# Six transposing DMAs per context in place of three, each issued after its predecessor has landed

## What is computed

```python
Pn = rmsnorm(P, input_norm_w)
k_proj, v_proj = Pn @ Wk.T, Pn @ Wv.T
for _ in range(3):
    q_proj = rmsnorm(slots, slot_norm_w) @ Wq.T
    scores = einsum('bkd,bmd->bkm', q_proj, k_proj) * SCALE
    attn = softmax(scores, axis=-2)
    attn = attn / (sum(attn, axis=-1) + EPS)
    slots = gru_cell(einsum('bkm,bmd->bkd', attn, v_proj), slots, ...)
```

## Time and profile before

| What | Value |
|---|---|
| median of 3 runs | 926.16 us (922.39 to 926.95) |
| span of the profiled execution, first to last instruction | 920.0 us |
| mean granted TensorE clock | 0.931 |
| PE busy | 771.6 us, 84% of the span |
| DVE busy | 599.2 us, 65% |
| ACT busy | 365.1 us, 40% |
| SP's DMA queue | 168272 packets, 100.85 MB |

### The profile page before, as it was taken

One profiled execution on the slowest core, in us unless ns is written; L12 is line 12 of the kernel. 1 busy time (PEld: TensorE's weight loads), 2 busy tenths in 40 slices (PEclk: granted clock), 3 DMA queues, 4 the chain that ended last, 5 costly groups with the idle time before them and its releaser, 6 DMA issues. The chain is left out here.

```text
span 920.0 us, 37878 instructions
## 1 busy us (share of the span) xinstructions
PE 771.6 (84%) x17278; PEld 644.6 (70%) x17278; DVE 599.2 (65%) x1152; ACT 365.1 (40%) x732; POOL 161.6 (18%) x431
## 2 busy tenths in 40 slices
PE   5697689998979998979998989888689886749995
PEld 2545579898979998969998979787644764324442
DVE  3886446875866776766875775645565878783325
ACT  3874415333534333524333521101247763352321
POOL 3021110311320411320311311101001013140003
PEclk9898889999988999999999999989889788779998
DMA  9977970346192346192355290601394701543424
GB/s 339 379 151 135 254 132 5 55 80 178 14 202 98 56 75 183 26 186 102 56 81 178 36 200 9 138 6 41 101 372 114 227 21 24 196 142 93 122 78 149
DMA packets 179419, 115.75 MB, mean 126 GB/s; under 512 B 145788, under 2 KB 158132, under 8 KB 176060
## 3 DMA queue, kind: packets, MB, share of 16 engines
q1 hardware_dynamic: 168272, 100.85, 43.2%
q10 hardware_dynamic: 8988, 6.69, 2.4%
q0 software_dynamic: 2000, 5.80, 2.2%
HBM read 61.94 MB, written 12.85 MB: 81 GB/s over the span
## 5 line engine op out<-in xcount | busy, mean ns | idle before, releaser
L1036 PE MATMUL banks<-qa,ctxT 128*128 128x64 f16 x3744 | 124.3, 197 | 26.7 <-issue 14.4
L1036 PEld LDWEIGHTS banks<-qa,ctxT 128*128 128x128 f16 x3744 | 120.5, 101 | 28.9 <-issue 15.3
L987 PEld LDWEIGHTS banks<-wall,whhT 128*128 128x128 f16 x3456 | 110.5, 99 | 14.9 <-issue 7.9
L987 PE MATMUL banks<-wall,whhT 128*128 128x64 f16 x3456 | 113.0, 195 | 7.9 <-issue 6.4
L987 PE MATMUL banks<-qa,wall 128*128 128x64 f16 x3456 | 104.9, 193 | 3.1 <-DVE qa L787 2.8
L987 PEld LDWEIGHTS banks<-qa,wall 128*128 128x128 f16 x3456 | 102.5, 98 | 3.4 <-DVE qa L787 3.0
L1055 PE MATMUL banks<-qa,wall 128*128 128x64 f16 (+1 forms) x1872 | 91.6, 197 | 7.1 <-issue 5.7
L1055 PEld LDWEIGHTS banks<-qa,wall 128*128 128x128 f16 (+1 forms) x1872 | 90.9, 101 | 7.8 <-issue 7.8
L1055 PE MATMUL banks<-wall 128*128 128x64 f16 (+1 forms) x936 | 90.4, 197 | 0.0
L1055 PEld LDWEIGHTS banks<-wall 128*128 128x128 f16 (+1 forms) x936 | 86.1, 101 | 0.0
L552 ACT ACTIVATE wall<-wall 128x832 f32<-128x832 f32 x24 | 21.5, 897 | 141.3 <-DVE wall L749 141.3
(11 more groups left out here) (279 smaller groups left out, 1490.9 us busy)
## 6 DMA issues: line engine op xcount, KB each, us to landing
wall<-in_ctx_dram SPq DMA_DIRECT2D x17, 1024.0 KB, 10.5
wall<-in_L_ffn_routed_w_dram SPq DMA_DIRECT2D x23, 512.0 KB, 8.3
unit<-in_ctx_dram SPq DMA_DIRECT2D x6, 1024.0 KB, 7.6
xg_scratch<-room SPq DMA_DIRECT2D x1, 3840.0 KB, 20.7
y_scratch<-room ACTq DMA_DIRECT2D x15, 256.0 KB, 2.0
ctxT<-in_L_xattn_gru_wih_dram SPq DMA_DIRECT2D x3, 1024.0 KB, 17.5
ctxT<-in_L_xattn_gru_whh_dram SPq DMA_DIRECT2D x1, 3072.0 KB, 26.1
ctxT<-in_L_attn_Wqkv_dram SPq DMA_DIRECT2D x12, 256.0 KB, 7.2
```

The source lines that it names most:

```text
L987: mm = pe.matmul(dst[o], a, b, start=start, stop=True, skip_group_check=True)
L1036: mm = pe.matmul(score[n][:, t * K:(t + 1) * K], a, q, start=(k == 0), stop=(k == 3 * DC - 1), skip_group_check=True)
```

## The change

`TURNS` gets six pieces of 5, 4, 4, 4, 5 and 4 halves. Each piece after the first waits until the one before has landed. The second and third load of a context wait for the landing of the one before (for contexts from 2 on). The load of x is waited for before the next is issued, the slots' load before `Wqkv`; the twelve loads of `Wqkv` go out in pairs, each pair after all earlier ones have landed.

```diff
-TURNS = ((0, 9), (9, 17), (17, HALVES))
+TURNS = ((0, 5), (5, 9), (9, 13), (13, 17), (17, 22), (22, HALVES))
...
             def load_context(b, groups=(0, 1, 2)):
                 n_rows = dram.ctx[b]
+                before = 3 * (b // 3) - (b > 3 and b % 3 == 1)
                 for j in groups:
+                    if b >= 2 and j >= 1:
+                        sp.wait_ge(ctx_in[b % 3], 16 * (before + j))
...
                     sp.wait_ge(tile_low, b * MT + lows)
+                    if g >= 1:
+                        sp.wait_ge(tile_turned[n][g - 1], 16 * (b // 2 + 1))
...
             sp.dma_start(rows, ...).then_inc(big.x_in, 16)
+            sp.wait_ge(big.x_in, 16)
...
             sp.wait_ge(scored[0], PAIRS * ITERS)
+            sp.wait_ge(big.res_in, 16)
             load_wqkv(sp, dram, big)
...
         for ii in range(4):
+            if ii % 2 == 0 and 4 * s + ii >= 2:
+                sp.wait_ge(big.wqkv_in, 16 * (4 * s + ii))
```

## The result

The kernel after took 960.2 us, the median of 4 runs (959.53 to 964.35), against 924.27 us (918.74 to 926.95, 4 runs) for the kernel before: a ratio of 1.0393, 95% interval 1.0353 to 1.0433. The forecast was 955, with a range of 930 to 976. The medians differ by only 36: the profiled execution of the kernel after is the slowest of its four, 4.2 us above their median. Runs of one kernel differ by several us, so terms of 1 or 2 us in a single trace are not firm.

What follows compares the result with a forecast made beforehand. It took PE to be bound by "issue" stops (29.2 us) and by SP deliveries without slack. Start-up +16, even contexts +3, odd +16, context 7 +3 and Wqkv -9 gave +29 us, so 955, range 930 to 976.

Steps and rivals of the forecast that it cites:

- What bounds: PE's stops in the recurrence: 29.2 us of "issue", read as waits for instructions, and waits for SP's deliveries, which lack slack.
- The price of a piece: SP's transposes: 0.61 us issue per half plus a tail of 2.6 per piece; six chained take 32.0 us (28.4 to 37.4).
- The price of a load: Context loads: 1 MB takes 5.6 us alone; three in a chain 17.0 us, against 13.4 side by side.
- Start-up, +16: Contexts 0 and 1: context 0's chain makes `scores(0, 1)` end 6.3 us later; `scores(1, 1)` ends at 156.2, before 140.1.
- What a stop does to PE's clock afterwards I leave at nothing: Whole kernel: PE's clock after a stop priced at zero, since stops stand there before and after.
- Even contexts, +3: Contexts 2, 4, 6: chained loads end at 225.5 instead of 221.9, delaying ACT's squares and cast; 1 us each.
- Odd contexts 3 and 5, +16: Chained pieces delay the next context's loads, ACT's gates and `slot_squares(0)`, which PE waits for; 8 us each.
- Context 7, +3: Last context, no loads behind it: the last piece lands 4.3 us later, costing 3 us (0 to 8).
- Loads waited for: ACT's waits for context loads: at seven places rather than four, 4 to 10 us each.
- Wqkv, -9: Wqkv loads in pairs let instructions between: PE's stops of 2.16 and 4.31 us and 3.4 of half clock go.
- The sum: Whole kernel: 16 + 3 + 16 + 3 - 9 = +29 us on a span of 920.0, giving a time of 955.
- the waits change nothing, only the splitting is left, within 4 us: Rival for the whole kernel: counts waited for already reached, no tail between pieces, within 4 us of 926; chance 0.07.

Runs made afterwards that it cites:

- e1: Kernel before with six pieces in place of three, no wait added: 908.2 us, 0.987 of the kernel before.
- e5: Kernel after without the waits between pieces and between loads (six pieces, Wqkv pairs, waits for x and slots stay): 905.1 us, 0.9797 of the kernel before.
- e8: e1, but PE waits for the six pieces two at a time, where it waited in the kernel before: 911.4 us, 0.9865 of the kernel before.
- e9: e5 with eleven pieces in place of six, no waits between them: 899.8 us, 0.973 of the kernel before.
- e11: Kernel after without the waits between the loads of a context; pieces still chained: 936.4 us, 1.0149 of the kernel before.
- e2: e1 with each piece waiting for the one before; loads and Wqkv as in the kernel before: 942.6 us, 1.0246 of the kernel before.
- e7: Kernel after without waits between pieces of contexts 0 and 1 and between loads of context 2: 936.4 us, 1.0125 of the kernel before.
- e10: Kernel after without the waits between pieces; loads still chained: 915.1 us, 0.9897 of the kernel before.
- e12: Kernel after without the waits between the loads of context 2; all other waits stay: 955.4 us, 1.0354 of the kernel before.

## Why the forecast was right, and where it was not

**What bounds: right.** SP's deliveries had no slack, and what was made later was paid for. The sign of every term was right. Whether the path of each term was right is told below; for the odd contexts it was not, in large part.

**The price of a piece: right.** The issues and landings of `turn_context`, all 48 pieces, then the six of context 0:

```profile
DMA to landing us min/median/max: 4.2/4.9/9.0
```

```profile
L364 SPq DMA_TRANSPOSE ctxT<-wall x6: 1611/1872/3147, 53.8 to 78.4; - x6
...
DMA to landing us min/median/max: 4.3/4.6/5.7
```

The chain of context 0 took 78.4 + 4.3 - 53.8 = 28.9 us (28.4 forecast). SP's timeline at start-up and around context 3:

```profile
90.45 23.21 SPq L398 DMA_TRANSPOSE whhT<-ctxT  x2
113.71 12.11 SPq L348 DMA_DIRECT2D unit<-in_ctx_dram  x3
125.99 5.57 SPq L364 DMA_TRANSPOSE ctxT<-wall  x1
```

```profile
228.22 11.35 SPq L348 DMA_DIRECT2D wall<-in_ctx_dram  x3
...
267.07 28.92 SPq L364 DMA_TRANSPOSE ctxT<-wall  x6
296.05 10.21 SPq L348 DMA_DIRECT2D wall<-in_ctx_dram  x3
```

The issues of context 3 ended 28.9 us after the first went out (29.4 forecast: 276.5 - 247.1). What I had wrong is the split between issue and tail: alone in the queue, four halves were often issued in 1.9 us, not 2.4, and the tail was the longer. The sum is the same. The price of a load held too: from the first issue of a chain of three to the first square of ACT that waited for it, contexts 3 to 7 took 14.8 to 17.3 us (17.0 forecast).

**Start-up, +16: it was 20.2, and the step that failed is "What a stop does to PE's clock afterwards I leave at nothing".** PE's timeline after (`scores(0, 1)`, then the fold), and the same fold before:

```profile
78.40 1.46 PE L1043 MATMUL banks<-qa,ctxT 128*128 128x64 f16 x24 [3.04 <-DMA ctxT<-wall]
82.81 2.10 PE L1043 MATMUL banks<-qa,ctxT 128*128 128x64 f16 x36 [2.96 <-DMA ctxT<-wall]
...
84.73 6.92 PE L961 MATMUL banks<-unit,wall 128*128 128x512 f16 x24
```

```profile
75.16 5.34 PE L954 MATMUL banks<-unit,wall 128*128 128x512 f16 x24
```

I priced the last three tiles at 3 x 0.36 = 1.1 us; after 3 us of waiting they took 2.10, and the fold behind them 1.6 more than before. The windows of the kernel after (us; busy PE, PEld, DVE, ACT, POOL; granted clock, DMA share, GB/s) have the reason, a clock granted at half, 1.2 GHz:

```profile
72.40:75.30 2.90, 2.90 (x97) 2.83 (x95) 2.23 (x4) 2.33 (x5) 0.00 (x0) 1.00 1.04 102
78.40:79.90 1.50, 1.46 (x24) 1.29 (x24) 0.00 (x0) 0.00 (x0) 0.00 (x0) 0.50 0.18 38
82.80:85.00 2.20, 2.19 (x37) 2.05 (x38) 0.05 (x1) 0.00 (x0) 0.00 (x0) 0.50 0.00 0
```

The Trainium skill describes this (TensorE: Matmul & The Clock Gate, HAM oscillation): a wait for a DMA between matmuls lets the clock fall, and the matmuls behind it run slow. Here the trace agrees: before, with no such wait, `scores(0, 1)` ran through in 4.71 us. So here a wait of 3 us cost PE more than its own length. Over the span busy time grew by 15.9 us; the sum had no such term. In the first stretch the miss was 11.5 - 6.3 = 5.2 us. Slower matmuls are 2.9 of it: 1.0 in the three tiles, 1.6 in the fold, 0.3 in `update`. The other 2.3 are the chain, whose last piece released PE at 82.81 and not at 80.5: the first piece went out at 53.8, as before, and not 1.7 earlier. (In e1, e5, e8, e9 and e11 it went at 51.7 to 52.1, in e2, e7, e10 and e12 at 53.4 to 53.9; what decides that is open.) The loads of context 2 then started 11.8 us later than before (6.3 forecast). What is queued behind their waits was right: `turn_context(1)` came 12.3 us after them (11.9 forecast), so at 126.0 and not near 120.

**Even contexts, +3: mis-sized, they cost 10.8.** The term rested on one context out of three. For context 2 it held (+0.8, 1 forecast). Context 4 shows what is different. ACT's timeline while context 5 is loaded, after and then before (squares L526, cast L563; before L519, L556):

```profile
381.94 0.90 ACT L559 ACTIVATE wall<-wall 128x832 f32<-128x832 f32 x1 [5.75 <-DVE wall L756]
...
391.37 0.63 ACT L526 ACTIVATE unit<-unit 128x512 bf16<-128x512 f32 x1 [8.53 <-DMA unit<-in_ctx_dram]
...
393.84 0.87 ACT L563 CAST qa<-wall 128x832 f16<-128x832 f32 x1
```

```profile
359.47 0.90 ACT L552 ACTIVATE wall<-wall 128x832 f32<-128x832 f32 x1 [10.11 <-DVE wall L749]
360.27 0.61 ACT L519 ACTIVATE unit<-unit 128x512 bf16<-128x512 f32 x1
...
362.85 0.89 ACT L556 CAST qa<-wall 128x832 f16<-128x832 f32 x1
```

By the end of the round before, the kernel after was 26.6 us behind; the exponential came only 22.5 later, since the "issue" stops of PE were gone, but the squares 31.1. Side by side the three loads of this context had landed 348.3 + 10.8 - 347.2 = 11.9 us after the first went out (not 13.4 as for context 3), and in the chain they took 385.9 + 5.4 - 374.8 = 16.5. PE then waits for DVE, DVE for ACT's cast, ACT for the loads (PE's timeline):

```profile
395.91 0.21 PE L1062 MATMUL banks<-qa,wall 128*128 128x64 f16 x1 [6.20 <-DVE wall L777]
```

In this stretch PE was idle 2.8 us longer in all (before, it stood still 4.6 us for "issue"), and busy 2.9 longer, at a granted clock of 0.90 instead of 1.00. The sentence that gained stops "give nothing back" here was right; the size of what stands in their place was not. Context 6 is another case: its wait for the low part was only 1.6 us, but PE's "issue" stops there rose from 3.5 to 6.9. The forecast had no such term, and it may differ from run to run.

**Odd contexts 3 and 5, +16: the size is right (14.1), the path only in part, so there is luck in it.** The forecast path exists. In context 3 ACT waited 7.94 us for the loads of context 4, and the gates of lane 0 came at 317.18, 25.4 us later than before. But PE was already 21.0 behind, so that is 4.4 and not 8. `slot_squares`, on which the whole term was put, waited only 1.4 us longer in the stretch of context 3 and 2.4 in that of context 5. The rest of context 3's 5.6 us are waits for pieces (+2.2, which the forecast held to add nothing), for the query (+1.2) and for the low part (+1.2). In context 5, 5.9 of the 8.5 us are the clock again, which was left at nothing (windows before and after: us; PE busy; granted clock, DMA share, GB/s):

```profile
371.09:462.22 91.13, 81.14 (x2617) 1.00 0.44 93
```

```profile
403.35:503.01 99.66, 87.04 (x2617) 0.91 0.45 90
```

**Context 7, +3: right,** 4.1; PE's last wait for a piece of context 7 was 4.5 us.

**Loads waited for: right in kind.** ACT's squares, seven waits forecast, six found:

```profile
ACT wall L526 <- DMA wall<-in_ctx_dram: 41.4, 5, 10.1
...
ACT unit L526 <- DMA unit<-in_ctx_dram: 8.5, 1, 8.5
```

They were 16.5 us in four and are 49.9 in six.

**Wqkv, -9: right in kind, -6.4.** The stops of 2.16 and 4.31 us are gone, and 8.3 came back up to `update(0, 12)`. The sum's 3.4 for the half clock was too much: it took all 6.8 us of the window, but PE was busy in 4.81 of them, which makes 2.4, and 8.9 in all. The pairs were in flight longer (SP's timeline, the issue of twelve, 6.16 us before):

```profile
632.36 23.23 SPq L1164 DMA_DIRECT2D ctxT<-in_L_attn_Wqkv_dram  x12
```

The last two went out at 654.8 and 655.2 and landed 3.4 to 4.0 us later. `update(1, 11)`, in which PE ran without a break before, took 1.9 longer with stops of 0.2 to 0.5 us. All eight kernels with pairs lose 1.7 to 2.5 us there and the others nothing, so it belongs to the pairs; that it is the price of the longer flight is argued, not shown.

**The sum** was +29 to the span and 955. The span grew by 42.6, the medians by 36. By the table 13.8 us were missed: the even contexts are 7.8, start-up 4.2, Wqkv 2.6 and context 7 1.1; the odd contexts were 1.9 too high. The clock runs through several of these terms: the busy time, forecast only as 3.4 us back, grew by 15.9. That the split itself gains 13 us was not seen either: it lies inside the terms, since they priced the pieces with their waits as a whole. As a rival, "the waits change nothing, only the splitting is left, within 4 us" was wrong by that.

## What to carry to other kernels

Splitting a transfer and waiting for its parts are two changes, and here they have opposite signs: small pieces start when less is ready (six alone: 0.987), each landing waited for adds a tail to a chain (the same six with waits: 1.025). Keep the pieces, and spend waits only where the queue's depth stops another engine and the data has slack, as at Wqkv (0.992). When a wait is put on the path of PE, price its length and the matmuls behind it at the lower clock. And test each term by its own path in the trace: a term can have the right size by another way, as with the odd contexts.

## What the runs showed of the hardware that was not expected

The time to issue four transposed halves is not fixed: in context 0 of the kernel after it was 1.6 to 1.9 us, in context 1 half of the pieces took 2.9 or more; the median landing was 4.6 us in both. What makes the difference was not tried. Splitting itself was nearly free in SP's queue around context 3: 22.43 us for six issues (e1) against 21.45 for three. And busy time of PE times the mean granted clock lay between 717 and 723 us in all 14 profiled kernels of this study, so that here the clock's part of a change could be read off the page. Last, the longer stops of PE for "issue" were, in this kernel, waits for blocks of instructions.
